# A fused state-space and expert kernel on one core: where GpSimd's angle products and weights, and VectorE's fractions, stand in the order of a step

## What is computed

```
def _get_kernel(log_dt, C, log_A_real, A_imag, length):
    ...
    P = dtA[:, :, None] * jnp.arange(length, dtype=jnp.float32)
    Cs = Cc * (jnp.exp(dtA) - 1.0) / A
    K = 2.0 * jnp.einsum('hn,hnl->hl', Cs, jnp.exp(P)).real
...
y = jnp.fft.irfft(u_f * k_f, n=n)[..., :Lq]          # causal convolution, u masked
y = y + u_m * D[:, None]
...
logits = jnp.einsum('bsd,ed->bse', x, route_w)
topk_v, topk_idx = jax.lax.top_k(logits, 1)
h = jnp.einsum('bsd,erd->bser', x, A)
out = jnp.einsum('bser,eor->bso', route_weight[..., None] * h, Bw)
x = x + out
```

## Time and profile before

| | us |
|---|---|
| median of 3 runs | 593.33 (591.96 to 594.21) |
| the profiled execution's own time | 591.81 |
| its span | 590.0 |
| PE busy | 562.4 (95% of the span) |
| DVE busy | 494.2 (84%) |
| POOL busy | 452.1 (77%) |
| ACT busy | 380.7 (65%) |

### The profile page before, as it was taken

The page is one execution under the profiler, slowest core; times in us unless marked ns, Lnnn a source line. Parts: engine busy times, 40 slices in busy tenths (PEclk is TensorE's granted clock), DMA queues, the critical chain, the costliest instruction groups (busy, mean ns, idle before and its releaser), DMA issues.

```text
span 590.0 us, 14019 instructions
## 1 busy us (share of the span) xinstructions
PE 562.4 (95%) x3400; PEld 501.8 (85%) x3400; DVE 494.2 (84%) x1408; ACT 380.7 (65%) x1245; POOL 452.1 (77%) x629
## 2 busy tenths in 40 slices
PE   4799999999999999999999999999999999999996
PEld 4688898988888898898988889899888889889985
DVE  7878888888889888888888888888888888888885
ACT  4777766666676666667667676666767666676630
POOL 5877888778787887878788788877878787787640
PEclk9999999999999999999999999999999999999999
DMA  7135545545645654654554564564565565466522
GB/s 153 51 71 167 153 129 167 175 110 166 177 114 160 176 137 139 175 154 125 170 166 116 169 172 118 159 178 130 146 174 124 149 177 149 129 172 177 135 91 101
DMA packets 107313, 85.61 MB, mean 145 GB/s; under 512 B 81944, under 2 KB 90586, under 8 KB 107234
## 3 DMA queue, kind: packets, MB, share of 16 engines
q1 hardware_dynamic: 97634, 51.19, 37.5%
q10 hardware_dynamic: 9600, 33.53, 14.2%
HBM read 51.02 MB, written 33.65 MB: 144 GB/s over the span
## 4 chain that ended last, share of the span: by engine, by line
PE 61%; DVE 19%; issue 10%; POOL 3%; ACT 2%; ACTq 2%; DVEq 0%; POOLq 0%
PE psYo L1262 13%; PE psZ L1288 12%; PE psYe L1262 10%; PE psS L1262 7%; DVE psS L1097 6%; PE psO L1366 4%; PE psO L1368 4%; PE psO L1371 4%; DVE ost L1136 3%; PE psXe L1276 2%; PE psXo L1276 2%; PE psZ L1355 2%; DVE Sf L1101 2%; ACTq L774 1%; PE psO L1319 1%
## 5 line engine op out<-in xcount | busy, mean ns | idle before, releaser
L1097 DVE SCALAR_TENSOR_TENSOR psS<-Sf,tab,psS 64x128 f32<-64x128 f32 x256 | 91.9, 359 | 59.3 <-ACT Sf L787 52.8
L1288 PE MATMUL psZ<-Wt,Y 128*128 128x136 f32 x1024 | 129.2, 279 | 0.0
L1288 PEld LDWEIGHTS psZ<-Wt,Y 128*128 128x128 f32 x1024 | 123.3, 190 | 0.1
L609 POOL TENSOR_TENSOR Slo<-Sf,Shi 128x384 fp32r<-128x384 f32 x64 | 64.8, 1013 | 72.1 <-ACT Shi L792 72.1
L1136 DVE TENSOR_TENSOR ost<-psO,xt 128x512 f32<-128x512 f32 x127 | 84.6, 683 | 0.8 <-PE psO L1371 0.7
L792 ACT ACTIVATE Shi<-Sf 128x384 fp32r<-128x384 f32 x64 | 33.6, 525 | 76.3 <-DVE Sf L1101 76.3
L553 POOL TENSOR_TENSOR both<-coarse,fine 128x512 f32<-128x512 f32 x64 | 67.7, 1058 | 1.3 <-ACT fine L693 1.2
L595 POOL TENSOR_TENSOR Xlo<-xeven,Xhi 128x384 fp32r<-128x384 f32 (+1 forms) x63 | 64.8, 1029 | 0.0
L717 ACT ACTIVATE cross<-Grev,tabm 64x256 f32<-64x256 f32 x118 | 59.7, 506 | 2.6
L573 POOL TENSOR_TENSOR Wg<-same,cross 128x256 f32<-128x256 f32 x59 | 43.1, 730 | 21.4 <-issue 18.7
L579 POOL TENSOR_TENSOR Glo<-Grev,Ghi 128x256 fp32r<-128x256 f32 x64 | 47.2, 737 | 15.7 <-ACT Ghi L700 15.4
(11 more groups left out here) (220 smaller groups left out, 1590.9 us busy)
## 6 DMA issues: line engine op xcount, KB each, us to landing
xt<-in_x_dram SPq DMA_DIRECT2D x64, 512.0 KB, 4.8
out_dram<-ost ACTq DMA_DIRECT2D x62, 512.0 KB, 5.1
Traw<-kdram SPq DMA_DIRECT2D x64, 128.0 KB, 2.9
xblk<-in_x_dram SPq DMA_DIRECT2D x480, 16.0 KB, 3.1
kdram<-krow SPq DMA_DIRECT2D x59, 1.5 KB
A_nat<-in_L_ffn_A_dram ACTq DMA_DIRECT2D x1, 512.0 KB, 4.1
B_nat<-in_L_ffn_Bw_dram SPq DMA_DIRECT2D x8, 64.0 KB, 3.0
out_dram<-ost SPq DMA_DIRECT2D x2, 256.0 KB, 2.5
```

The costliest lines, as they stand in the source:

```text
L609: pool.tensor_tensor(Slo[h.s2][:, :], Sf[h.s2][:, :], Shi[h.s2][:, :].bitcast(F32), ALU.subtract).then_inc(slo_done, 1)
L1097: dve.scalar_tensor_tensor(psS[to, new], Sf[h.s2][fr, old], tab2[fr, BR, h.n:h.n + 1], psS[to, new], ALU.mult, ALU.add).then_inc(brought_d ...
L1288: last = pe.matmul(psZ[:, 0:NW], Y[:, j, c, :], Wt[:, 2 * c + j, :], start=(j == 0 and c == 0), stop=(j == 1 and c == NE - 1), skip_group_ ...
```

## The change

Nothing is added or taken away; four pieces of work change their place.

1. GpSimd: `angle_steps` of a part moves from i mod 4 = 0 to the next step, i mod 4 = 1, behind `g_table` and ahead of `s_lo`. For the part that begins at head 8 it moves from the prologue into step 1, ahead of `g_table` there.
2. GpSimd: `weigh` stays in i mod 4 = 0 but moves behind `g_table`.
3. VectorE: `whole_turns` and `high_fraction` move from behind the carry of a step with i mod 4 = 2 to the end of the step before; `low_fraction` and `clamp` likewise from i mod 4 = 3 to the end of the step before.
4. VectorE, prologue: `x_lo` of head 1 ahead of `carry` of head 0.

```diff
@@ GpSimd, step
                 if head(2).there and not with_matrix(head(2)):
                     w_table(head(2))
-                if part_at(head(8)):
-                    angle_steps(part_at(head(8)))
+                if head(3).there and not is_head(head(0), 1):
+                    g_table(head(3))
+                if part_at(head(7)) and not is_head(head(0), 1):
+                    angle_steps(part_at(head(7)))
                 if part_at(head(4)):
                     weigh(part_at(head(4)))
-                if head(3).there and not is_head(head(0), 1):
-                    g_table(head(3))
                 if head(0).there:
                     s_lo(head(0))
...
                 if is_head(head(0), 1):
+                    angle_steps(part_at(head(7)))
                     g_table(head(3))
                     g_lo(head(2))
@@ GpSimd, prologue
             g_lo(first[2])
-            angle_steps(parts[2])
             run_steps(step)
@@ VectorE, step
                 if head(0).there:
                     carry(head(0))
-                if part_at(head(6)):
-                    whole_turns(part_at(head(6)))
-                    high_fraction(part_at(head(6)))
-                if part_at(head(5)):
-                    low_fraction(part_at(head(5)))
-                    clamp(part_at(head(5)))
...
                     if not is_head(head(0), H - 1):
                         add(head(-1), 1)
+                if part_at(head(7)):
+                    whole_turns(part_at(head(7)))
+                    high_fraction(part_at(head(7)))
+                if part_at(head(6)):
+                    low_fraction(part_at(head(6)))
+                    clamp(part_at(head(6)))
@@ VectorE, prologue
+            x_lo(first[1])
             carry(first[0])
-            x_lo(first[1])
```

## The result

| | before | after |
|---|---|---|
| median, 20 runs each | 593.23 us (591.74 to 595.54) | 594.71 us (594.32 to 596.65) |
| the profiled execution's own time | 591.81 | 594.54 |
| its span | 590.0 | 592.7 |

The ratio of after to before is 1.0034, 95% interval [1.0024, 1.0043]: a third of a per cent slower, inside the 0.5% that I had called no change. The forecast median was 594.6. That it is so close is partly luck. The profiled execution of after lies 0.2 us under its median and that of before 1.4 under, so the difference of own times, on which the sum was made, is +2.7 us, where the sum said +1.3. The 25 runs of the kernel before that stand beside the experiments go by their mean granted clock: those at 1.00 took 591.8 to 592.3 us, those at 0.991 took 594.1 to 594.7.

A forecast was written before the change was run, and what follows sets the result against it. TensorE was taken as the bound, plus 0.94 us lost per step i mod 4 = 0 and 0.30 per i mod 4 = 3. Terms -12.2 + 4.8 - 4.2 + 5.7 + 8.8 - 1.6 = +1.3 gave 594.6 us, range 585 to 599.

The forecast's parts named there:

- 1. GpSimd, i mod 4 = 0: GpSimd's `angle_steps` leaves and `weigh` fits into the wait for `Shi`: the 0.94 us loss goes in thirteen steps, -12.2 us.
- 2. GpSimd, i mod 4 = 1: `angle_steps` ahead of `Slo` makes TensorE start at 6.28 instead of 5.91: loss 0.37 us, thirteen times, +4.8.
- 3. VectorE: Fractions leave their old place, -4.2 us; ahead of the carry they wait for `Wg` and `both`, +5.7 and +8.8.
- 4. Start: Prologue: TensorE's 2.64 us idle goes, less 1.08 for `angle_steps` in step 1 ahead of `g_table`: gain 1.6 us.
- No pair slipped ahead: Rival, 15%: in i mod 4 = 3 VectorE's pair comes ahead of GpSimd's `Wg`, carry on time, 8.8 us less, 585.8.
- The hidden case: Rival, 11%: no blocking in the fractions' new place ahead of the carry; they are hidden, -13.2 us, 580.1.
- GpSimd is barely pushed back: Rival, 16%: VectorE's slipped-in instruction delays `both` and every carry behind it; 27 steps at 0.15 give +4.0 us, 598.6.

The follow-up runs named there:

- PSUM version: The changed kernel, order untouched, with `whole` and the result of `low_fraction` written into a free PSUM bank: 579.22 us, ratio 0.9769 to the kernel before.

## Why the prediction came out as it did

**1. GpSimd, i mod 4 = 0: the number right, its cause only in part.** Forecast loss 0, measured 0.00; -12.2 stands. But the forecast gave the 0.94 to GpSimd alone, and that is not so. With part 3 made and GpSimd's order as before, 0.60 is left; with GpSimd's parts made and the fractions put back, 0.20. So the whole of it goes only because part 3 is made as well.

**2. GpSimd, i mod 4 = 1: right to 0.02.** Forecast for this step: `Wg` at 1.57, `Slo` at 5.17, TensorE at 6.28. Measured from the first `psS` matmul at 242.43: 1.58, 5.17 and 6.28. The windows give 0.40, in all 5.3 us over thirteen steps for the forecast 4.8. With `angle_steps` elsewhere the loss is gone.

**3. VectorE: the mechanism right, the size 2.6 us too small.** The fractions are blocked by `Wg` and `both`, and through PSUM they are not. The carry of i mod 4 = 2 began at 2.32 for 2.31, that of 3 at 2.64 for 2.50. The mis-sized term is the second, the carry of i mod 4 = 3: `both` took 1.10 where I had 1.06, and the carry begins 0.03 behind a blocked instruction, where I had it overlap the end by 0.07 as in undisturbed rows; together that is the 0.14. In i mod 4 = 2 the same 0.10 was cancelled because `Wg` began at 0.39 and not at 0.48. By the windows the losses are 0.48 and 0.79, in all 6.3 us in thirteen steps and 10.8 in fourteen, for 5.7 and 8.8; of the fourteen, step 3 lost only 0.58 (9.00 for 8.42), because `Wg` starts there at 0.50 and not at 0.73.

**4. Start: 1.05 us too small, the other way.** I took 2.64 - 1.08 = 1.6; it is 2.65. The projection of head 0 moves from 34.29 to 31.26, 3.03: 1.54 of it idle time (2.64 became 0.64 and 0.46), some 1.25 the granted clock, which no longer falls, and 0.24 a difference that stands ahead of the move (head 0's `psS` at 21.28 for 21.52; it varies from 21.2 to 21.8 over the kernels), which is luck. The window behind it shrinks by 0.72 (9.72 to 9.00), because GpSimd's prologue has lost `angle_steps`, and only the next, 8.65 to 9.75, pays the 1.10 that was forecast as 1.08. The term left out is the clock, and the prologue's windows of before show it: 0.51 from 28 to 30 us.

So the terms in the steps were 0.5 + 0.6 + 2.0 = 3.1 us too small, and 0.2 us are left in i mod 4 = 0; the 0.9 us that before lost in its 57 steps beyond the regular losses, and that I had left as they were, are inside these measured sums; and the start is 1.05 better. 3.3 - 0.9 - 1.05 makes +1.35, between the +1.3 of the sum and the +2.7 measured. The errors lie on both sides, so that the forecast 594.6 met 594.71 is luck in part.

**The rivals.** No pair slipped ahead in the 13 regular rounds: each of the four instructions varies by at most 0.08 us (`low_fraction` 0.79 to 0.87). The hidden case (580.1) is what the PSUM version makes true, 579.2. GpSimd is barely pushed back: `both` grows from 1.06 to 1.10 us in i mod 4 = 3 and hardly in 2 (1.05 to 1.08), under the 0.065 from which that rival was to decide.

## What to carry to other kernels

Before work of VectorE is moved into a gap, look at what GpSimd does in that gap, and not only at the gap's length: here 0.57 us of work in SBUF became 1.46 us. Where the gap can't be chosen, choose the operands: one side in a PSUM bank that is free at the moment takes the instruction out of the collision. The price here was a wait for the additions that read the bank: `whole` starts 0.11 us behind them instead of 0.09 ahead of their end, which the slack took in. And work out the slack of the chain behind the gap first, since one number (here 1.87 us for the carry) then prices every version; read it in steps whose other losses are known, because the largest loss of a step hides the next one.

## What the runs showed of the hardware that was not expected

- A blocked VectorE instruction does not need its own length once GpSimd's is over. It ends a nearly fixed time behind it, 0.08 us for `TENSOR_SCALAR` and 0.15 for `SCALAR_TENSOR_TENSOR` of 128x128 fp32, less than their own 0.28 and 0.29. I know of no row that says whether it had begun before or is that fast; it stays open.
- The exclusion is lopsided here. `Wg` and `both` stand back to back on GpSimd, and the VectorE instruction that `Wg` held up ends when `both` has already started. `both` is longer by 0.04 to 0.06 us when that instruction is a `SCALAR_TENSOR_TENSOR` with two SBUF inputs (1.10 to 1.12 in 13 rounds each: i mod 4 = 3 in after and through PSUM, both kinds of step with `angle_steps` behind `Tlo` and the fractions in SBUF), and by 0.03 at most when it is `whole` (1.05 to 1.08).
- 2.64 us without a matmul were followed, 1.3 to 1.8 us behind the first matmul, by a stretch of some 3 us at the lower granted clock in both kernels that have that idle time (0.50 with part 4 undone, 0.51 in the same window of before); two gaps of 0.64 and 0.46 us were not. That the gap is the cause rests on this: the same one move of `Xlo` takes both away, in either kernel.
